# Sums over neighbours: fewer groups by slots, more gathered chunks, other buffers and banks

## The reference

```python
def _sage_conv(h, src, dst, W_l, b_l, W_r, num_nodes):
    msgs = h[src]
    agg = jax.ops.segment_sum(msgs, dst, num_segments=num_nodes)
    deg = jax.ops.segment_sum(jnp.ones((src.shape[0],), h.dtype), dst, num_segments=num_nodes)
    mean = agg / jnp.maximum(deg, 1.0)[:, None]
    return mean @ W_l + b_l + h @ W_r
h = jax.nn.relu(_sage_conv(x, src, dst, W1_l, b1_l, W1_r, n))
out = jax.nn.relu(_sage_conv(h, src, dst, W2_l, b2_l, W2_r, n))
```

## Time and profile before

| | |
|---|---|
| median of 3 runs | 9221.45 us (9193.35 to 9228.59) |
| the profiled execution, its span | 9219.16 us, 9217.4 us |
| TensorE matmul / weight load busy | 7101.9 / 6261.9 us |
| VectorE, ScalarE, GpSimd busy | 6545.3, 3179.6, 4540.8 us |
| L1820, gather by slots (both passes) | 8232 matmuls |
| L1832, sum by target (both passes) | 8232 matmuls |
| L1800, chunk sums | 2016 matmuls |
| L1765, chunk gathers | 672 indirect DMAs, 1026.5 us busy, mean 1528 ns |

### The profile page before, as it was taken

How to read it: one execution, slowest core, us unless ns; L and a number is a source line. 1 busy time by engine, 2 the same in 40 slices (tenths; PEclk the granted TensorE clock), 3 DMA queues, 4 the chain that set the end, 5 groups by cost and what they waited for, 6 DMA issues and landing times. The chain is left out here.

```text
span 9217.4 us, 249498 instructions
## 1 busy us (share of the span) xinstructions
PE 7101.9 (77%) x84292; PEld 6261.9 (68%) x84292; DVE 6545.3 (71%) x18880; ACT 3179.6 (34%) x6051; POOL 4540.8 (49%) x3929
## 2 busy tenths in 40 slices
PE   6577566666666999999977999799975666666666
PEld 6344566666666888898876888688864555555555
DVE  3899444444435999999986888488864777777775
ACT  1000111111123666666654666366631111111111
POOL 1788777777710000000003666166633777777774
PEclk9676788888857999999997999699975665555665
DMA  5412333333303323322322334133422222222221
GB/s 62 58 42 43 95 100 103 100 101 102 100 21 93 93 93 92 93 93 93 92 70 80 102 102 102 54 101 102 103 61 38 51 49 51 50 50 51 51 51 41
DMA packets 718460, 697.33 MB, mean 76 GB/s; under 512 B 394630, under 2 KB 523494, under 8 KB 717864
## 3 DMA queue, kind: packets, MB, share of 16 engines
q1 hardware_dynamic: 590488, 539.53, 21.5%
q0 software_dynamic: 125776, 150.49, 8.7%
q10 hardware_dynamic: 1728, 0.25, 0.0%
HBM read 639.21 MB, written 50.66 MB: 75 GB/s over the span
## 5 line engine op out<-in xcount | busy, mean ns | idle before, releaser
L805 POOL DMA_INDIRECT soft_G<-soft,soft_idx x1568 | 1599.2, 1020 | 540.7 <-issue 475.6
L805 POOL DMA_INDIRECT msg_G<-msg_src,msg_idx x1176 | 1229.9, 1046 | 364.4 <-issue 353.2
L1765 POOL DMA_INDIRECT sage_chunk_rows<-sage_rows,chunk_src x672 | 1026.5, 1528 | 756.8 <-PE ps L1800 435.4
L669 POOL MEMSET acc<- 96x1280 f32 x30 | 34.4, 1162 | 2570.4 <-POOLq L2192 2260.9
L1809 ACT ACTIVATE sage_G<-ps 128x384 bf16<-128x384 f32 (+1 forms) x2100 | 1018.0, 485 | 682.4 <-PE ps L1820 677.8
L1820 PE MATMUL ps<-T,sage_ohT 128*128 128x192 bf16 x8232 | 1041.8, 248 | 29.4 <-DVE sage_ohT L1732 28.1
L1612 PE MATMUL ps<-att_far,att_ohT 128*128 128x65 bf16 x15582 | 925.9, 194 | 172.0 <-DVE att_ohT L1551 112.4
L1738 DVE TENSOR_SCALAR sage_ohd<-iota,sage_cols 128x256 bf16<-128x256 bf16 x4116 | 917.2, 284 | 198.8 <-PE ps L1832 195.3
L1832 PE MATMUL ps<-sage_G,sage_ohd 128*128 128x192 bf16 x8232 | 1020.1, 245 | 1.9 <-issue 1.9
L1612 PE MATMUL ps<-acc,att_ohT 128*128 128x65 bf16 x15582 | 921.2, 194 | 0.0
L1933 PE MATMUL ps<-ident,soft_G 128*128 128x128 f32 x1568 | 379.4, 422 | 694.1 <-DMA soft_G<-soft,soft_idx 694.1
(11 more groups left out here) (463 smaller groups left out, 14793.0 us busy)
## 6 DMA issues: line engine op xcount, KB each, us to landing
sage_rows<-srow SPq DMA_DIRECT2D x336, 320.0 KB, 3.4
acc<-pair_rows SPq DMA_DIRECT2D x196, 448.0 KB
att_rows<-pair_rows SPq DMA_DIRECT2D x147, 448.0 KB, 3.8
msg_edge<-edge_attr SPq DMA_DIRECT2D x196, 256.0 KB
msg_row<-dst_rows SPq DMA_DIRECT2D x196, 256.0 KB
soft_row<-dst_rows SPq DMA_DIRECT2D x196, 256.0 KB
soft_G<-soft,soft_idx POOLq DMA_INDIRECT x1568
sage_rows<-srow SPq DMA_DIRECT2D x84, 288.0 KB
```

The lines of the kernel that those rows point to most:

```text
L669: done(pool.memset(acc[0:TOP, nodes], 0.0), "zeroed")
L805: eng.indirect_dma_start(B["G"][h][:, j, :], None, src_table, bass.IndirectOffsetOnAxis(ap=B["idx"][h][:, j:j + 1], axis=0)).then_inc(gath ...
L1765: pool.indirect_dma_start(chunk_rows[n % 2][:, j, :], None, sage_rows, bass.IndirectOffsetOnAxis(ap=chunk_src[:, n, j:j + 1], axis=0)).the ...
```

## The change

42 groups by slots become 32, 42 chunks become 80 (`NC`), five for two groups. A chunk begins at every tenth step, its eight parts in the first eight of the ten. Rows, offsets and one-hots of chunks have five buffers each (two before), the loaded source rows have two (five before). The turned sums go to the bank in which the group was summed (5 or 6) in place of bank 7; `pe_turn` no longer waits for the last adds, and `pe_sum` waits before a group's first step for the add of the group before last in place of its reduce. The chunk's add has lag 32 in place of 33. `chunk_iota` keeps 256 columns and is read four times over. The indirect DMAs, the matmuls of a chunk and their sizes are the same.

```diff
-XG = 42
+XG = 32
+XC = 5
+XSTEP = 10
+    NC = XG // 2 * XC
-                chunk_in = gathered[0:2]
-                rows_in = [scope.enter_context(nc.semaphore(f"{name}_rows_in{k}")) for k in range(RING)]
+                chunk_in = gathered[0:XC]
+                rows_in = [scope.enter_context(nc.semaphore(f"{name}_rows_in{k}")) for k in range(2)]
-                        rows, ohT = buf("rows", [P, 2 * BATCH * P], BF16, RING), buf("ohT", [P, 2, 2 * BATCH * P], BF16)
+                        rows, ohT = buf("rows", [P, 2 * BATCH * P], BF16), buf("ohT", [P, 2, 2 * BATCH * P], BF16)
-                        chunk_rows, chunk_off = buf("chunk_rows", [P, TPC, 3 * D], BF16), buf("chunk_off", [P, TPC], BF16)
-                        chunk_oh = buf("chunk_oh", [P, TPC // 2, P, 2], BF16)
+                        chunk_rows, chunk_off = buf("chunk_rows", [P, TPC, 3 * D], BF16, XC), buf("chunk_off", [P, TPC], BF16, XC)
+                        chunk_oh = buf("chunk_oh", [P, TPC // 2, P, 2], BF16, XC)
+                        def turned(k):
+                            return ps[0:D, 5 + k, 0:SB]
+                        def chunk_of(i, s):
+                            return i * XC + s // XSTEP, s // XSTEP, s % XSTEP
 ...
-                                need(sp, S["ohT"], nb - RING + 1)
+                                need(sp, S["ohT"], nb - 1)
 ...
-                            dve.wait_ge(S["cadd"], g + 1)
+                            need(dve, S["cadd"], i * XC + (2 if s < STEPS else 4))
-                            dve.tensor_tensor(w, w, ps[0:D, 7, 0:SB], ALU.add).then_inc(S["added"], 1)
+                            dve.tensor_tensor(w, w, turned(s // STEPS), ALU.add).then_inc(S["added"], 1)
-                            for n in range(XG):
-                                need(pool, S["csum"], n - 1)
+                            for n in range(NC):
+                                need(pool, S["csum"], n - XC + 1)
 ...
-                            need(dve, S["coh"], n - 1)
+                            need(dve, S["coh"], n - XC + 1)
-                            need(dve, S["csum"], n - 1)
+                            need(dve, S["csum"], n - XC + 1)
-                            dve.tensor_tensor(chunk_oh[k][:], chunk_iota[:], pairs, ALU.is_equal).then_inc(S["coh"], 1)
+                            dve.tensor_tensor(chunk_oh[k][:], chunk_iota[:].broadcast_to([P, TPC // 2, P, 2]), pairs, ALU.is_equal).then_inc(S["coh"], 1)
-                            need(dve, S["added"], n)
+                            need(dve, S["added"], i * 2 + (0, 0, 1, 1, 2)[s // XSTEP])
 ...
-                            n, k, j = i * 2 + s // STEPS, s // STEPS, s % STEPS
+                            n, k, j = chunk_of(i, s)
-                                need(pe, S["added"], n)
 ...
-                                need(pe, S["red"], g - 1)
+                                need(pe, S["added"], g - 1)
 ...
                             pe.wait_ge(S["red"], g + 1)
-                            need(pe, S["added"], g)
-                            pe.wait_ge(S["cadd"], g + 1)
-                                ins = pe.transpose(ps[0:D, 7, half * P:(half + 1) * P], red[s // STEPS][:, half, :], ident[:])
+                                ins = pe.transpose(turned(s // STEPS)[:, half * P:(half + 1) * P], red[s // STEPS][:, half, :], ident[:])
-                                flow(dve, (0, dve_one_hots), (18, dve_chunk), (11, dve_reduce), (21, dve_add), (33, dve_chunk_add))
+                                flow(dve, (0, dve_one_hots), (18, dve_chunk), (11, dve_reduce), (21, dve_add), (32, dve_chunk_add))
 ...
-        chunk_iota = chunks_kept.enter_context(nc.sbuf_tensor("chunk_iota", [P, TPC // 2, P, 2], BF16))
+        chunk_iota = chunks_kept.enter_context(nc.sbuf_tensor("chunk_iota", [P, 1, P, 2], BF16))
```

More of the change, by code:

```diff
@@ L1727, in dve_one_hots @@
                             if q % BATCH == 0:
-                                nb, ring, b, w = batch(i, s)
-                                dve.wait_ge(rows_in[ring], (g + 1) * 16)
+                                nb, b, turn, w = batch(i, s)
+                                dve.wait_ge(rows_in[b], turn * 16)
                                 need(dve, S["gathered"], n - BATCH)
                                 for half in range(2):
-                                    ins = dve.tensor_scalar(ohT[b][:, half, 0:w], rows[ring][:, 0:w], iota_p1[:, half:half + 1], None, ALU.is_equal)
+                                    ins = dve.tensor_scalar(ohT[b][:, half, 0:w], rows[b][:, 0:w], iota_p1[:, half:half + 1], None, ALU.is_equal)
                                 ins.then_inc(S["ohT"], 1)
@@ L1784, in dve_chunk_add @@
                             dve.wait_ge(S["csum"], n + 1)
-                            need(dve, S["added"], n)
+                            need(dve, S["added"], i * 2 + (0, 0, 1, 1, 2)[s // XSTEP])
                             need(dve, S["cadd"], n)
                             w = acc[0:D, bass.ds(first, P)]
-                            dve.tensor_tensor(w, w, ps[0:D, 7, SB:SB + P], ALU.add).then_inc(S["cadd"], 1)
+                            dve.tensor_tensor(w, w, ps[0:D, 7, 0:P], ALU.add).then_inc(S["cadd"], 1)
@@ L1799, in pe_chunk @@
                             for part in range(3):
-                                ins = pe.matmul(ps[0:D, 7, SB:SB + P], chunk_rows[k][:, j, part * D:(part + 1) * D], chunk_oh[k][:, j // 2, :, j % 2],
+                                ins = pe.matmul(ps[0:D, 7, 0:P], chunk_rows[k][:, j, part * D:(part + 1) * D], chunk_oh[k][:, j // 2, :, j % 2],
                                                 start=(j == 0 and part == 0), stop=(j == TPC - 1 and part == 2))
```

38 lines of the change are left out of this document (19 added, 19 removed).

## The result

| | before | after |
|---|---|---|
| median (range, runs) | 9205.76 us (9187.51 to 9228.59, 12) | 9232.28 us (9213.23 to 9243.27, 12) |
| ratio | | 1.0032, 95% interval 1.0021 to 1.0042 |
| the profiled execution, its span | 9219.16 us, 9217.4 us | 9243.27 us, 9241.5 us |
| the two passes, first gather's start to last add | 841.8, 844.4 us | 853.9, 861.8 us |

Slower by 0.32%. That is under the 0.5% that the prediction took for the least that can be told from none; with 12 executions of each it can be told. The passes alone are 12.1 + 17.4 = 29.5 us longer, of 173 forecast; all other stretches together lost 5. As the chunk gathers are L1765 before and L1775 after, the other lines of interest are now L1742 and L1748 (comparisons), L1809 (chunk sums), L1829 and L1841 (gather and sum by slots), L1787 (a chunk's one-hot), L1798 (its add).

The account below looks back on a forecast made before the run. TensorE (99% busy) bounds the passes before, GpSimd after: 640 x 1.4425 = 923 us, 928.4 with the ends against 841.8, so +86.6 a pass, +173 in two; 9219.2 + 173 = 9392, median 9394, range 9275 to 9560.

Parts of the forecast that it names:

- TensorE's part: TensorE's work in each of the two passes falls from 833 to 788 us, 90 us less for the program.
- Who takes over: In the passes GpSimd, at 50.0 us or more for two groups against TensorE's 49.3, becomes the bound.
- The sign: The program gets slower, chance 0.82; it comes out level at a mean gather duration of 1.00 us.
- The small parts: Row buffers, turned sums' bank, chunk's add, chunk_iota: nothing or hidden; masks, column loads and semaphores under 2 us.
- seven of a chunk's eight DMAs at 1.00 us and one at 2.1, so 1.14: Mean duration of GpSimd's chunk gathers in the passes; 1.44 us each with the gap.
- the chunk's add at lag 32: VectorE's wait for the chunk's last matmul costs 0 to 0.5 us a chunk, inside GpSimd's lateness.
- GpSimd hardly held up: Rival: gathers in the passes take 0.945 to 1.0 us, program 73 us shorter (9149) at best; chance 0.16.
- The clock drops: Rival: TensorE's idle waits for rows lower its clock in the passes, program 9673; chance 0.09 together with rival (3).
- Every comparison holds GpSimd up: Rival: all VectorE comparisons delay gathers, 1.45 us each, program 9787; chance 0.09 together with rival (2).
- held up as now: Rival: gathers in the passes still take 1.53 us, program 9900; chance 0.01.
- The signs looked for: In the passes: GpSimd never waiting for TensorE, TensorE waiting 1 to 2 us for most chunks, gathers 1.05 to 1.30 us.
- TensorE busy 85%: Sign: in the changed kernel's passes TensorE, waiting for the chunk's rows, is busy some 85%.

Follow-up runs that it names:

- experiment 1: Changed kernel with every second chunk gather left out, TensorE reading each gathered block twice (sums not the reference's): ratio 0.9886 to the kernel before, 9108.37 us.
- experiment 8: Kernel before with only the turned sums moved to the group's own bank, with the waits of the change: ratio 1.0001.
- experiment 6: Kernel before with VectorE waiting for its own last pair of comparisons before each step's next pair: ratio 1.0099.
- experiment 2: Changed kernel with one more pair of 1280-column comparisons on VectorE before each such pair: ratio 1.0031 to the kernel before.
- experiment 5: Kernel before with a single-column addition on VectorE in front of every step's comparisons: 9285.65 us against 9206.82, one execution.
- experiment 7: Changed kernel with VectorE waiting for its own last pair of comparisons before each step's next pair: ratio 0.9956 to the kernel before, 9155.75 us.
- experiment 3: Changed kernel with a pair of two-input VectorE ops (tensor_tensor) added before each pair of 1280-column comparisons: ratio 1.0062 to the kernel before.
- experiment 4: Changed kernel with a single-column addition on VectorE in front of every step's comparisons: ratio 1.0065 to the kernel before.
- experiment 12: Changed kernel with 34 groups and 69 chunks, VectorE waiting for its own last comparisons in each step: ratio 0.9896 to the kernel before, 9112.19 us.

## Why the prediction was wrong

**What held.** *TensorE's part*: 788 us a pass without its ends, 797 with them; measured 790 with them when half of the gathers are left out (experiment 1). *Who takes over*: GpSimd, with no wait for TensorE's sums and a gap of 0.305 us; its pass is its 640 start-to-start times and a tail of 5.5 us, both as forecast. *The sign*: slower, but by a narrow margin. The break-even was a mean of 1.00 us and the runs gave 1.028; with a term that was off by 0.11 the sign owes something to luck. *The small parts*: the bank is worth 1.0001 (experiment 8); VectorE waited for loaded rows twice in both passes, 8.9 us, at their starts, so two row buffers cost nothing.

**The step that failed** is the one term "seven of a chunk's eight DMAs at 1.00 us and one at 2.1, so 1.14". Measured: 1.028 us. The difference is 0.11 us, times 1280 it is 141 us, of the 149 us between the forecast for the profiled execution (9392) and its 9243.27. The rest: the second pass before took 844.4 us and not the 841.8 of the first, and the stretches outside the passes lost 5. The range ended at 9275, 43 us above the median; it let in a mean of 1.05 us at the least.

The term has two parts. One gather in eight was to be held up, 160 of 1280 at 2.1 us; 59 were (1.3 us and more), at a mean of 1.96. The other seven were put at 1.00 us and took 0.983. So of the 141 us some 111 lie in how many gathers are held up, 22 in the price of the free ones and only 7 in what a held one costs.

Why it was too high. The prediction let the burst of each chunk (its one-hots, a pair of long comparisons, its add) catch one gather. How often a burst catches one had been read from no row; the price came from the stretches without a gap, where the whole mean is 1.90 us. Matching the rest of the round by VectorE's busy share gave 1.00 us, nearly the right value, but the share is not the reason: the kernel before and experiment 6 have the same share, 84%, with means of 1.53 and 1.01 us, and at 94% it is 1.01 (experiment 2).

What goes with the mean is how long VectorE works without a stop. Call a stretch unbroken while each instruction starts before the last one has ended, and take the mean of its length over VectorE's busy time in the passes. It is 4.6 us in the kernel before and 2.4 in the changed one, where VectorE stops for every chunk's add and when TensorE waits for rows. In the three kernels with 4.5 to 5.8 us (before, experiments 5 and 8) a gather takes 1.50 to 1.54 us; in the eleven with 1.5 to 2.9 us it takes 0.98 to 1.11. Experiments 6 and 7 move the length by a pause alone, 4.6 to 1.7 us and 2.4 to 1.6, and the mean follows.

The length is no price for a single gather, though (all counts are over both passes of the traces). In the kernel before 447 of 672 gathers had 0.945 us and more of unbroken work ahead when they began. Of these 156 took 1.3 us and more, of the other 225 none: two in three got through in the middle of the comparisons. In the changed kernel it was 42 of 449, and 17 of the other 831. With 2 us and more ahead the mean is 2.06 us before, 1.14 after and 0.95 in experiment 2. And of the 132 gathers of 1.7 us and more in the kernel before 78 ended without any stop of VectorE since they began. So a stop takes the long gathers away, but it isn't the only thing that ends one, and what picks out the gather that is caught is open.

**The edit priced as nothing that mattered** was the chunk's add at lag 32: "0 to 0.5 us a chunk, inside GpSimd's lateness". VectorE waits there 1.06 us (70.1 us in 66 times). Before it waited there too, 0.63 us (22.0 us in 35), but once in 25 steps and not in ten. It costs no time on the path, but it is a stop that breaks VectorE's stretches. That this wait itself, and not the one at L1841 (107.5 us in 168), keeps the mean at 1.03 is argued and not shown: no run moved the add alone.

**The rivals.** (1) *GpSimd hardly held up*, level at a mean of 1.00 us: the nearest. The mean is 1.028, a few hundredths on the slow side of that point; experiment 7 with 0.979 lies on its fast side, and that program is faster than before (0.9956), so the point was placed well. The chance of 0.16 that it was given can't be judged by one outcome. (2) *The clock drops*: it did, in small. Two neighbouring windows after, in the columns of the earlier trace rows:

```profile
5101.40:5104.80 3.40, 3.40 (x22) 2.61 (x22) 0.48 (x2) 0.74 (x2) 2.71 (x3) 0.51 0.21 43
5104.80:5108.00 3.20, 3.20 (x36) 2.42 (x33) 2.90 (x10) 1.31 (x4) 2.29 (x4) 1.00 0.15 31
```

The lower level (1.2 GHz) is granted in 13 short stretches after, beside those at the passes' starts and ends. TensorE had stood idle for 2.1 to 4.2 us shortly before each, as here, where it waited 3.98 us for rows until 5101.37; of its 18 waits of 2 us and more before the passes' ends 13 were followed by such a stretch. In the passes before there is none but at their starts and ends. TensorE is busy for 794.93 and 798.91 us against 786.05 and 787.73 for the same 8256 matmuls in experiment 7, where the clock stays at 0.99: 9 to 11 us a pass. In the changed kernel they lie inside the time that TensorE would spend waiting for rows anyway, as the pass is GpSimd's sum without them. (3) *Every comparison holds GpSimd up*, 9787, and (4) *held up as now*, 9900: both fell, as they need means of 1.45 and 1.53 us and the runs gave 1.028.

The Trainium skill (SBUF — State Buffer, Who interferes with whom) says that the engine which starts second is blocked for the whole instruction. The held gathers of 2 to 6 us agree in kind. But they last over many instructions of VectorE, back to back, as if the next one got in again before GpSimd; no run shows that step itself. And with pauses most gathers take 0.94 to 0.95 us (median 0.946 in experiment 6) although comparisons still run beside them. As a price for each comparison the rule gave 1.45 us and the runs 1.03.

**The signs looked for.** GpSimd without waits: right. TensorE waiting 1 to 2 us for most chunks: wrong. It waited for the rows of 92 of 160 chunks, for 65 of them under 1 us, for 6 as forecast and for 21 longer. TensorE busy 85%: wrong, 93%, by the same error in the pass. Mean of 1.05 to 1.30: wrong, just under.

**What stays open.** What decides whether a gather that meets unbroken work of VectorE is caught, one in three in the kernel before and one in eleven in the changed one. The order in which both engines start may fall into step in a loop that repeats; that is argued, no run shows it. That experiment 2 holds GpSimd no more than the changed kernel fits its unbroken stretches, which are no longer (2.2 against 2.4 us), but no run added comparisons without adding stops. Also open is why experiments 3 and 4 are 0.3% slower than the changed kernel by their medians, while the passes of the profiled executions are within 3 us of its own in sum: in these executions the extra 30 and 18 us lie outside the passes. The profiled execution of the changed kernel (9243.27 us) is the slowest of its 12, so one execution's passes don't settle differences of this size.

## What to carry to other kernels

When an engine takes over as the bound, the forecast hangs on its start-to-start time, and a duration that depends on a neighbour must be priced by how often it is caught and for how long. Count that in the rows; here it went with how long the neighbour works without a stop, and not with the neighbour's busy share. With 1280 repeats a tenth of a microsecond is 1.4% of this program. If GpSimd's gathers are late beside comparisons, a wait of VectorE for its own last op, at 0.15 us, is worth trying wherever VectorE has time and GpSimd has none; where TensorE then waits for VectorE, as in experiment 6, it costs more than it gives. And divide work so that the engine with the fixed cost stays a little below the other: 32 gathers for two groups gave 1%, 40 lost it all, and with the pauses gave 0.4%.

## What the runs showed of the hardware

A gather of 128 rows costs GpSimd 0.94 us and a gap of 0.305 us, 1.25 us from start to start, 0.944 being the median over 1280. Beside unbroken comparisons on VectorE it took up to 6.19 us, though two in three that began there were not held up; with a pause every two comparisons it never took over 1.59 in experiments 6 and 7, and 2.08 in experiment 12. A single-column addition between the comparisons left the mean where it was (1.50 and 1.53 us). A wait of VectorE for its own last comparison costs 0.15 us. After 13 of TensorE's 18 waits of 2.1 to 4.4 us for rows the granted clock was 0.5 for 3.4 to 6.8 us.
